# Second attention: bounding and squaring two neighbouring tiles of weights in one VectorE operation

## The reference

```python
def _shepards_mha(Q, K, V):                       # 16 heads of 16, 1024 tokens, 4 batches
    sq = q2 + jnp.swapaxes(k2, -1, -2) - 2.0 * jnp.einsum('bhqd,bhkd->bhqk', Q, K)
    dist = jnp.sqrt(jnp.maximum(sq, 0.0))
    W = (SHEP_EPS + dist) ** (-2)                 # SHEP_EPS = 1e-4
    W = W / (SHEP_EPS + jnp.sum(W, axis=-1, keepdims=True))
    return jnp.einsum('bhqk,bhkd->bhqd', W, V)
```

## Time and profile before

| | us |
|---|---|
| three runs | 3926.96, 3935.29, 3931.84 (median 3931.84) |
| the profiled execution, its own time | 3926.37 |
| its span in the profile | 3924.5 |
| DVE busy, of the span | 2560.2 (65%) |
| ACT busy, of the span | 2220.2 (57%) |
| PE busy, of the span | 3426.8 (87%) |

### The profile page before, as it was taken

How to read it: one execution, slowest core, us unless ns; L and a number is a source line. 1 busy time by engine, 2 the same in 40 slices (tenths; PEclk the granted TensorE clock), 3 DMA queues, 4 the chain that set the end, 5 groups by cost and what they waited for, 6 DMA issues and landing times. The chain is left out here.

```text
span 3924.5 us, 55078 instructions
## 1 busy us (share of the span) xinstructions
PE 3426.8 (87%) x21412; PEld 2521.5 (64%) x21412; DVE 2560.2 (65%) x4350; ACT 2220.2 (57%) x2873; POOL 1042.7 (27%) x924
## 2 busy tenths in 40 slices
PE   4999999889999999977767777767767999999998
PEld 3555555478888899963333333333326888889998
DVE  5777777554433455548999999999995443335554
ACT  1666666543222344427998998998993322233443
POOL 3333233100122012125552552551320002200212
PEclk7999999999999999988878878878878999999999
DMA  3000000010010134330000000000001001013342
GB/s 123 1 1 1 1 1 1 1 65 6 29 37 28 39 117 105 95 77 1 1 1 1 1 1 1 1 1 1 1 1 65 6 22 37 24 45 91 93 111 40
DMA packets 86805, 124.88 MB, mean 32 GB/s; under 512 B 7767, under 2 KB 73257, under 8 KB 86544
## 3 DMA queue, kind: packets, MB, share of 16 engines
q1 hardware_dynamic: 68880, 100.18, 7.5%
q0 software_dynamic: 17664, 21.17, 3.2%
HBM read 85.15 MB, written 42.55 MB: 33 GB/s over the span
## 5 line engine op out<-in xcount | busy, mean ns | idle before, releaser
L1851 DVE TENSOR_TENSOR b_w<-b_w 128x2048 f32<-128x2048 f32 x256 | 583.3, 2309 | 24.0 <-ACT b_w L1929 15.9
L1888 ACT ACTIVATE b_w<-b_ring 128x1024 f32<-128x1024 f32 x512 | 481.8, 1051 | 94.9 <-PE b_ring L1971 94.7
L1929 ACT ACTIVATE b_w<-b_w 128x2048 f32<-128x2048 f32 x256 | 468.1, 1897 | 1.4
L1401 ACT ACTIVATE f2hid<-f2ring 128x512 f32<-128x512 f32 (+2 forms) x256 | 132.3, 517 | 577.4 <-PE f2ring L1481 560.4
L1401 ACT ACTIVATE f1hid<-f1ring 128x512 f32<-128x512 f32 (+2 forms) x256 | 132.4, 517 | 576.5 <-PE f1ring L1481 559.5
L1319 DVE TENSOR_TENSOR f2hid<-f2hid,f2ring 128x512 f32<-128x512 f32 (+2 forms) x256 | 150.1, 586 | 439.7 <-ACT f2hid L1401 439.5
L1319 DVE TENSOR_TENSOR f1hid<-f1hid,f1ring 128x512 f32<-128x512 f32 (+2 forms) x256 | 150.1, 586 | 439.2 <-ACT f1hid L1401 439.1
L1959 PE MATMUL b_acc<-b_w,b_vg 128*32 128x512 f32 x2048 | 318.9, 704 | 127.3 <-DVE b_w L1851 126.6
L1795 DVE TENSOR_SCALAR b_w<-b_w 128x2048 f32<-128x2048 f32 x256 | 324.2, 1311 | 31.7 <-ACT b_w L1888 31.3
L625 ACT ACTIVATE a_prob<-a_wide 128x1024 f32<-128x1024 f32 (+1 forms) x320 | 292.6, 943 | 84.3 <-PE a_wide L731 58.2
L1481 PE MATMUL f1ring<-f1xh,f1wg 128*128 128x512 f32 (+2 forms) x1536 | 326.1, 354 | 10.3 <-DVE f1xh L1302 8.1
(11 more groups left out here) (342 smaller groups left out, 6913.1 us busy)
## 6 DMA issues: line engine op xcount, KB each, us to landing
X<-expert_in SPq DMA_DIRECT2D x16, 650.0 KB, 5.2
expert_in<-a_zeros SPq DMA_DIRECT2D x8, 650.0 KB, 9.8
X<-in_x SPq DMA_DIRECT2D x4, 1024.0 KB, 10.3
x_mid<-X SPq DMA_DIRECT2D x8, 512.0 KB, 3.1
f1raw_x<-in_rd SPq DMA_DIRECT2D x4, 1024.0 KB, 5.5
f1raw_xf<-in_rg SPq DMA_DIRECT2D x4, 1024.0 KB, 4.9
f1raw_xf<-in_ru SPq DMA_DIRECT2D x4, 1024.0 KB, 7.0
f1raw_g<-in_rg SPq DMA_DIRECT2D x4, 1024.0 KB, 4.9
```

What stands on the lines that cost most here:

```text
L1401: s_eng.activation(hid[:, s % 2, 0:n], slot(step)[:, 0:n], ACT.Silu).then_inc(s_silu, 1)
L1851: v.tensor_tensor(one(m), one(m), one(m), ALU.mult).then_inc(s_wts, 1)
L1888: s.activation(w[:, m, 2 * pair:2 * pair + 2, :].rearrange("p h n -> p (h n)"), slot(at + pair), ACT.Ln, scale=SHEP_EPS ** -2).then_inc(R. ...
L1929: s.activation(one(m), one(m), ACT.Sigmoid, scale=-0.5).then_inc(s_sig, 1)
```

## The change

Two tables say which tiles one DVE operation covers. The bounds are made of tiles (0,1), (2,3), (4,5), (6), (7), and the squares of tiles (0), (1,2), (3,4), (5,6), (7). So a half unit has 5 bounds and 5 squares in place of 8 and 8; six of the ten cover two tiles, 128x4096. Over the stage, 512 operations become 320. A pair of bounds stands where the second of its bounds stood, and a pair of squares where the first of its squares stood. A bound of a pair waits until both tiles' logs are done, a square of a pair until both sigmoids are. It adds 2 to its semaphore, at its end. The work between the squares stays tied to m.

```diff
+    BOUNDS = ((0, 2), (2, 4), (4, 6), (6, 7), (7, 8))
+    SQUARES = ((0, 1), (1, 3), (3, 5), (5, 7), (7, 8))
...
+        def run(first, end):
+            return w[:, first:end].rearrange("p m h n -> p (m h n)")
...
-                def bound(j, m):
-
-                    R.wait_free(dve, AT["dist", j, m] + PAIRS - 1 + SLOTS, ())
-                    v.tensor_scalar(one(m), one(m), LOG_MIN, None, ALU.max).then_inc(s_bound, 1)
+                def bound(j, first, end):
+
+                    for m in range(first, end):
+                        R.wait_free(dve, AT["dist", j, m] + PAIRS - 1 + SLOTS, ())
+                    v.tensor_scalar(run(first, end), run(first, end), LOG_MIN, None, ALU.max).then_inc(s_bound, end - first)
+
+                def squares(j, first, end):
+
+                    dve.wait_ge(s_sig, TB * j + end)
+                    v.tensor_tensor(run(first, end), run(first, end), run(first, end), ALU.mult).then_inc(s_wts, end - first)
...
                     for m in range(TB):
-                        dve.wait_ge(s_sig, TB * j + m + 1)
-                        v.tensor_tensor(one(m), one(m), one(m), ALU.mult).then_inc(s_wts, 1)
+                        for first, end in SQUARES:
+                            if m == first:
+                                squares(j, first, end)
...
                     for m in range(TB if j + 1 < PERIODS else 0):
-                        bound(j + 1, m)
+                        for first, end in BOUNDS:
+                            if m == end - 1:
+                                bound(j + 1, first, end)
```

More of the change, by code:

```diff
@@ L1841, in _ @@
                     operand(0, i)
-                for m in range(TB):
-                    bound(0, m)
+                for first, end in BOUNDS:
+                    bound(0, first, end)
                 for j in range(PERIODS):
```

## The result

The changed kernel takes 3988.76 us (median of 4 runs, 3988.01 to 3997.12) beside 3931.37 of the kernel before on the same chip: a ratio of 1.0148, 95% interval 1.0136 to 1.0159, or 57.4 us slower. The forecast was 3970 within 3943 to 3998. The direction was right and the time lies within the range, but the loss is 19 us larger than the 38.6 of the forecast.

A forecast was written before the change was run, and what follows sets the result against it. In the second attention it took a chain at DVE's pace, then ACT's, with square k + 3 releasing log k through PE, as the bound. Terms summed to 38.6 us, giving 3965, or 3970 on the median's base; range 3943 to 3998.

The forecast's parts named there:

- The pair (5,6) and log 2: Odd half units: log 2 starts 1.75 us behind the end of pair (5,6), so log 4 starts 1.0 us later.
- The third stack in plain odd half units: Third stack's last step, held behind pair (1,2), delays cast 2 by 0.5 to 0.7 us, bounds 0 and 1.0.
- 5, 13 and 21: Counted among 12 odd half units without a turn, at 1.7 us each; 5.1 us for these three.
- the rival on GpSimd: GpSimd's fourth stack loses to pair (3,4), waits 4.3 us; 12 half units give 24 more: 3994; chance 15%.
- 9, 17 and 25: Half units with a turn: four PE steps wait for pair (1,2) ahead of ACT's copy; 1.5 each, 4.5 us.
- 8, 16 and 24: Dist 1 waits for DVE's add, behind tile 6 in both kernels: -0.2 us each, -0.6 together.
- Behind the moments: Half units 10 and 18: pair of bounds (2,3) delays the moments, 0.9 beside 1.3 us each; 4.4 us.
- the even ones: Plain even half units (0, 6, 14, 22, 26, 28): later log 4, PE possibly late; 1.3 us each, 7.8.
- Half unit 30: In 30 and 31 pair (1,2) waits for sigmoid 2: 1.4 us less the savings, together 1.9.
- The saving: Each merged square saves 0.08 us; six merges per half unit give 0.48, 15 us over 31 half units.
- DVE's own time: Rival: DVE's time from square 0 to last bound decides, so merging is faster, 3917 or 3902 us; chance 6%.
- The clock rival: PE's clock falls to 1.2 GHz ahead of values 3 in most half units: 3998 us; chance 17%.

The follow-up runs named there:

- split squares: Changed kernel with each pair of squares as two single operations, a wait and signal per tile, order and paired bounds kept: 3950.43 us beside 3932.05.
- filled PE: Changed kernel with unread matmuls added on PE, two ahead of values 1, four ahead of values 3, two ahead of values 5: 3979.01 us beside 3933.95.
- the run without stacks: Changed kernel without GpSimd's work on the operand stacks from the second unit on, waits and signals kept: 3974.50 us beside 3930.58.

## Why the prediction held, and where it fell short

**The pair (5,6) and log 2: right, and shown.** Log 2 follows the pair by 1.73 in half unit 19 and by 1.74 with this pair alone, and split squares bring 35.76 back. With that pair alone the stage loses 37.9 us, two thirds of the whole, though part of that is PE's clock.

**The third stack in plain odd half units: right for the pair (1,2) alone, absent in the changed kernel.** The forecast gave 0.5 to 0.7 in each of them to a cast 2 that waits for the third stack, at most 1.0. With the pair (1,2) alone that wait is there, 1.08. In the changed kernel no cast of a plain odd half unit waits. GpSimd had started its stacks earlier there, and where a step was held behind the pair (1,2) it belonged to the fourth stack, which has time. The failed step is that the forecast took GpSimd's place in time from the kernel before. The class still came out near the forecast (17.1 to 15.3) through two other costs. In 19 the table load to log 2 takes 26.11 where the forecast had 31.00 - 5.44 = 25.56. Of these 0.55, 0.3 is the pair (1,2), which takes 4.59 to the cast behind it instead of 4.32, and each of two pairs starts 0.07 later behind a cast (1.42 after the cast's start, not 1.35 as in the earlier trace rows). In 3 and 15 the clock adds more. So the right size here was partly luck.

**5, 13 and 21: 14.8 instead of 5.1.** The failed step is that they were counted as plain odd ones. Their GpSimd is late behind the residual add. It was late in the kernel before as well, and merged bounds moved it back by 3 more us. The wait that the forecast had put into all twelve, and a step held for a whole pair as in the rival on GpSimd (4.3 us there, 4.42 measured), cost time in the changed kernel in these three alone, though at the second stack and casts 1 and 2, not at the fourth and cast 3. Leaving out the stacks takes 4.5 to 4.7 from each.

**9, 17 and 25: 13.5 instead of 4.5.** The mechanism was right (four steps behind one end, a copy ahead of three sigmoids). The failed step is the choice near the lower end, "because PE was at the full clock there". It was nearly so before in 9 and 25, but not in 17, where values 1, the fourth stack and values 2 took 1.93, 1.97 and 1.48. In the changed kernel PE waits 1.97 us ahead of the four, and in 9 three of them ran at 1.2 GHz. The filled PE gives 40.5, that is +1.6 each, just the 1.5 that the full clock was to give.

**8, 16 and 24: -3.2 instead of -0.6.** The clock has a share: before, both steps behind DVE's add in half unit 8, dist 1 and values 5, ran at the half clock, 1.22 and 1.93; after, they took 0.73 and 1.31, and only the next two were slow. How much of the 3.2 that is was not measured by itself.

**Behind the moments, the even ones, 4, 12 and 20: right** within 1 us for each class. **Half unit 30: wrong cause.** The forecast blamed the pair (1,2). With this pair alone it costs nothing; with merged bounds and single squares it costs 2.0, and PE's timeline of that run has values at 1.93 and dist at 1.22 behind a wait of 2.31 for ACT, where before values at 1.06 followed the same wait. The kernel before without stacks took 33.82 in it too. So it goes with the clock, whatever was merged.

**The saving.** DVE's busy time in the stage fell by 7.7 us, not by 15. A pair takes 4.34 to the next operation and not the 4.40 of two squares, so a saving of 0.06 stands, near the 0.08 of the forecast. Where the other half of the 15 went is not settled. Bounds stretched beside GpSimd, such as the three that take 9.09, are not it: in the kernel before a bound at that place took 5.58, and after 5.55. One part is the gating product (`b_gated`), 508 ns on average instead of 425, 2.6 us in all. The fixed latency of the Trainium skill (VectorE: DVE Perf Modes, on the TRN2 errata) fits the durations, 4.42 against 2 x 2.29, a difference of 0.16, but not the pace of the stream.

**The rivals.** DVE's own time does not decide: the changed kernel and the five versions that merge only some of its operations are all slower. The clock rival stood at 17% with 3998; the filled PE shows it at work to the extent of 12 us. GpSimd has 13.5 us, read from the run without stacks. The log chain and what goes with it keep some 30; that is what is left of 57.4 and not measured by itself, and the single costs do not simply add up. **Open** is what the pair (3,4) alone costs beyond the plain odd half units, and what decides whether PE has the full clock when a given pair ends: half units with the same instructions differ.

## What to carry to other kernels

Count what a merged operation holds back before what it saves: here a merge saved 0.06 us and made the first of its two tiles arrive 2.2 us later at an engine that works in order. Look then at who is idle while the longer operation runs: TensorE may come back at half its clock, and a step of GpSimd may take the whole length (4.42 us here instead of 0.24). In a schedule this tight, shortening one engine's work can lose time, so try order, size and clock apart.

## What the runs showed of the hardware

- A GpSimd step on 128x16 took 0.24 us unhindered (2005.21 in half unit 5) and 4.42 behind a DVE square of 128x4096. It works the other way too: a GpSimd add on 128x2048 and the DVE bound beside it stand in each other's way, and in half unit 5 the three bounds took 9.09 us, where the three took 4.56 unhindered (half unit 19). The add ended at 1991.00 and the bound held behind it, which takes 1.22 by itself, at 1992.09 after 5.55 us. The Trainium skill (SBUF — State Buffer, on the two separate sides of SBUF) states an exclusive lock for a port pair; both cases agree with it. The second was there in the kernel before too, where the bound took 5.58.
- TensorE took 1.94 us instead of 1.06 for the same eight matmuls behind some waits of 2 to 3 us, but not behind each: 1.93 behind 1.97 in half unit 9, 1.07 behind 2.16 in half unit 17. With 496 matmuls more in the stage the clock granted there rose from 0.78 to 0.85 and the kernel was 12 us faster. With less work for GpSimd in the kernel before, PE stood idle for 2.50 us in half unit 3 and then took 1.94, and that half unit was 1.0 us longer.
